# A graph network on one core: every third edge group permuted, a layer as one straight program, records in a ring

## The reference

```python
for l in range(6):
    W = ssp(edge_attr @ mlp_w1[l] + mlp_b1[l]) @ mlp_w2[l] + mlp_b2[l]   # ssp: softplus less log 2
    W = W * C[:, None]                       # cutoff from the edge's length
    xf = h @ conv_w1[l]
    msg = xf[src] * W
    agg = segment_sum(msg, dst, N)
    h = h + (ssp(agg @ conv_w2[l] + conv_b2[l]) @ lin_w[l] + lin_b[l])
x = layernorm(x + h)
for l in range(3):                           # second block
    z = (1 + eps[l]) * h + segment_sum(h[src], dst, n)
    h = relu(z @ W1[l] + b1[l]) @ W2[l] + b2[l]
```

## Time and profile before

| | |
|---|---|
| timed runs | 4567.78, 4573.64, 4575.24 us, median 4573.64 |
| profiled execution | span 6617.0 us |
| TensorE busy | 4785.2 us, 72% |
| its weight loads | 3558.4 us, 54% |
| VectorE | 3028.4 us, 46% |
| ScalarE | 2174.5 us, 33% |
| GpSimd | 2995.9 us, 45% |
| moved by DMA | 574.64 MB, 87 GB/s |

### The profile page before, as it was taken

How to read it: one execution, slowest core, us unless ns; L and a number is a source line. 1 busy time by engine, 2 the same in 40 slices (tenths; PEclk the granted TensorE clock), 3 DMA queues, 4 the chain that set the end, 5 groups by cost and what they waited for, 6 DMA issues and landing times.

```text
span 6617.0 us, 88816 instructions
## 1 busy us (share of the span) xinstructions
PE 4785.2 (72%) x24401; PEld 3558.4 (54%) x24684; DVE 3028.4 (46%) x8117; ACT 2174.5 (33%) x3585; POOL 2995.9 (45%) x3161
## 2 busy tenths in 40 slices
PE   0376777867777777777777777767777777777789
PEld 0365555645555555555555555545555555555544
DVE  3244444544444444444444444544444444444532
ACT  0133333333333333333333333333333333333322
POOL 5634444444454445444445444444445444445400
PEclk5687777777777777777777777777778777777799
DMA  4452233233233333233333323233333332323300
GB/s 157 137 151 84 83 86 88 82 91 85 82 87 85 85 90 89 80 86 86 86 86 91 85 84 88 85 85 87 85 85 88 86 89 84 86 84 87 87 14 9
DMA packets 324938, 574.64 MB, mean 87 GB/s; under 512 B 73578, under 2 KB 117300, under 8 KB 322996
## 3 DMA queue, kind: packets, MB, share of 16 engines
q1 hardware_dynamic: 202572, 357.07, 17.9%
q0 software_dynamic: 100160, 203.51, 11.5%
q10 hardware_dynamic: 21928, 11.64, 0.6%
HBM read 524.00 MB, written 47.93 MB: 86 GB/s over the span
## 4 chain that ended last, share of the span: by engine, by line
PE 40%; another core or an unknown queue 27%; issue 13%; DVE 10%; DVEq 4%; ACT 4%; POOL 2%; DMA 1%; ACTq 0%; SPq 0%; POOLq 0%
PE ps_w L680 10%; PE ps_h L781 9%; PE ps_a L695 8%; PE ps_a L692 4%; PE ps_pair L894 3%; POOL permuted L551 2%; DVE ex_msg L1428 2%; PE ps_pair L707 2%; DVEq L342 2%; ACT ps_w L1025 1%; DVE aggT L1409 1%; PE ps_a L669 1%; DVE phot L1388 1%; ACT xc L1062 1%
## 5 line engine op out<-in xcount | busy, mean ns | idle before, releaser
L561 POOL DMA_INDIRECT rows<-node_table,src_all x2982 | 2820.5, 946 | 3117.5 <-DVE ex_msg L1428 1937.8
L680 PEld LDWEIGHTS ps_w<-edge_w,hid 128*128 128x128 f32 x8064 | 1336.7, 242 | 1295.6 <-issue 1295.3
L680 PE MATMUL ps_w<-edge_w,hid 128*128 128x128 f32 x8064 | 1392.8, 329 | 719.0 <-ACT ps_w L1025 471.4
L1571 DVE SCALAR_TENSOR_TENSOR hid<-xc,ps_h 128x512 f32<-128x512 f32 x1008 | 690.9, 686 | 1859.5 <-remote 1328.5
L1060 ACT ACTIVATE xc<-ps_h 128x512 f32<-128x512 f32 x1008 | 601.3, 597 | 2648.2 <-remote 1363.6
L781 PE MATMUL ps_h<-buffers,edge_w 112*128 112x512 f32 x2016 | 1347.9, 756 | 86.4 <-DVE hid L1571 46.3
L695 PE MATMUL ps_a<-hot,ex_msg 128*128 128x32 f32 x6048 | 952.1, 306 | 469.7 <-issue 251.2
L695 PEld LDWEIGHTS ps_a<-hot,ex_msg 128*128 128x128 f32 x6048 | 887.8, 226 | 522.6 <-issue 512.8
L1062 ACT ACTIVATE xc<-xc,half_col 128x512 f32<-128x512 f32 x1008 | 727.3, 722 | 32.6
L1025 ACT COPY ps_w<-seed_rows 128x512 f32<-128x512 f32 x1008 | 591.6, 587 | 413.9 <-DVE ex_msg L1428 342.8
L1416 DVE TENSOR_TENSOR aggT<-aggT,ps_a 128x32 f32 x756 | 140.4, 186 | 927.2 <-remote 631.0
(11 more groups left out here) (236 smaller groups left out, 2825.5 us busy)
## 6 DMA issues: line engine op xcount, KB each, us to landing
buffers<-in_attr SPq DMA_DIRECT2D x756, 224.0 KB
buffers<-src_select SPq DMA_DIRECT2D x252, 256.0 KB
buffers<-attr_permuted SPq DMA_DIRECT2D x252, 224.0 KB
rows<-node_table,src_all POOLq DMA_INDIRECT x2982
permuted<-aggT SPq DMA_DIRECT2D x7, 1248.0 KB, 17.6
hid<-permuted SPq DMA_DIRECT2D x42, 208.0 KB
counts<-in_rec SPq DMA_DIRECT2D x4, 1924.0 KB, 35.4
hi_mid<-node_table SPq DMA_DIRECT2D x6, 1280.0 KB
```

Source lines behind the costliest of these rows:

```text
L561: pool.indirect_dma_start(out=rows[:, use % RS, t * F:(t + 1) * F], out_offset=None, in_=table[:, :], in_offset=bass.IndirectOffsetOnAxis( ...
L680: mm = pe.matmul(ps_w[u % 2][:, t * F:(t + 1) * F], hid[:, u % 2, t * P:(t + 1) * P], edge_w[:, EW_W2:EW_W2 + F], start=False, stop=(t == ...
L1571: dve.scalar_tensor_tensor(out=hid[:, i % 2, :], in0=xc[:, i % 2, :], scalar=LOG_MAX, in1=ps_h[i % 2][:, :], op0=ALU.min, op1=ALU.max).the ...
```

## The change

1. `M` is 3: every third group is permuted, 56 of 168 in a layer; 112 are gathered. The permuted tail of edges is 204 tiles, not 148, and 56 groups are turned in the prologue.
2. The loop over passes is gone: `U` = 168, and the engines' programs hold a whole layer, with constant addresses. The slice copies go. Early node chunks are tied to steps 72, 120 and 159, and the count tiles (27 groups of four in a layer, 28 before) are spread by `count_steps`, mostly over steps of unpermuted index.
3. `rows` has 7 slots; the edge features keep 4, now indexed apart from `M`; `select` keeps two, one for every other permuted group.
4. Records pass the scatter in a ring of three quarters of the tail: the load of the fourth quarter waits until the first is scattered. The zeroing is in 13 pieces.
5. For room, start tables (`pbase_i`, `block_i`, `base_i`, `pbase_kept`) share one buffer on different partitions, and `in_window` lies in `phot`.

```diff
-M = 4
-U = 24
+M = 3
+U = 168
-NIT = 7
-NP_GROUPS = NIT * J
-NQ_GROUPS = NIT * J * (M - 1)
+NP_GROUPS = J
+NQ_GROUPS = J * (M - 1)
-AS, RS = M, 6
+AS, RS = 4, 7
-CLEARS, REC_LOADS = 7, 4
+CLEARS, REC_LOADS, REC_RING = 13, 4, 3
-LEAD = M
-PRIME = 2
-EARLY_AT = [3, 5, 6]
+LEAD = 4
+PRIME = 4
+EARLY_STEP = [72, 120, 159]
-RANK_BLOCKS = 3
+RANK_BLOCKS = 2
-COUNT_STEP = [4, 4, 5, 6, 8, 9, 10, 11, 13, 13, 14, 15, 17, 18, 19, 20]
+def count_steps():
+    bounds, steps = [1] + EARLY_STEP + [U], []
+    room = [(end - first - 6) // 4 * 4 for first, end in zip(bounds, bounds[1:])][:EARLY]
+    wanted = [4 * round(BG * n / sum(room)) for n in room]
+    wanted[0] += BT - sum(wanted)
+    for first, end, n in zip(bounds, bounds[1:], wanted):
+        free = range(first + 3, end - 2)
+        light = [i for i in free if i % M]
+        heavy = [i for i in free if not i % M]
+        extra = n - len(light)
+        if extra > 0:
+            light += [heavy[j * len(heavy) // extra] for j in range(extra)]
+        else:
+            light = [light[j * len(light) // n] for j in range(n)]
+        steps += sorted(light)
+    return steps
+def group_of(use):
+    return use // (M - 1) * M + use % (M - 1) + 1
...
             for c in range(REC_LOADS):
-                part = slice(c * RT // REC_LOADS, (c + 1) * RT // REC_LOADS)
-                sp.dma_start(rec[:, part, :], rec_d[:, part, :]).then_inc(rec_in[c], 16)
+                first, end = REC_STARTS[c], REC_STARTS[c + 1]
+                if c >= REC_RING:
+                    wait_scattered(sp, c - REC_RING)
+                sp.dma_start(rec[:, c % REC_RING, 0:end - first, :], rec_d[:, first:end, :]).then_inc(rec_in[c], 16)
...
-            for t in range(RT):
-                if t in REC_STARTS:
-                    pool.wait_ge(rec_set, REC_STARTS.index(t) + 2)
-                    pool.sem_inc(gate, 1)
-                pool.indirect_dma_start(
-                    out=perm_d[:, :], out_offset=bass.IndirectOffsetOnAxis(ap=pos_i[:, t:t + 1], axis=0),
-                    in_=rec[:, t, :], in_offset=None).then_inc(scattered, 16)
+            for c in range(REC_LOADS):
+                pool.wait_ge(rec_set, c + 2)
+                pool.sem_inc(gate, 1)
+                for t in range(REC_STARTS[c], REC_STARTS[c + 1]):
+                    pool.indirect_dma_start(
+                        out=perm_d[:, :], out_offset=bass.IndirectOffsetOnAxis(ap=pos_i[:, t:t + 1], axis=0),
+                        in_=rec[:, c % REC_RING, t - REC_STARTS[c], :], in_offset=None).then_inc(scattered[c % REC_RING], 16)
...
+                    def gather_uses(first, last):
+                        for use in range(first, last):
+                            uses.wait(msg_done, group_of(use - RS))
+                            pool.sem_inc(gate, 1)
+                            gather_group(use, use, table_d[half])
...
                 with pe.Fori(0, K) as k:
-                    with pe.Fori(0, NIT) as it:
-                        uses = Uses(pe, layer * (K * NIT) + k * NIT + it).ready(-1, -5)
-                        early_step = load_early(pe, it)
-                        for i in range(U):
+                    uses = Uses(pe, layer * K + k).ready(-1, -5)
+                    for i in range(U):
+                        if i in EARLY_STEP:
+                            early_step = load_early(pe, EARLY_STEP.index(i))
...
-                                dve.tensor_scalar(phot[:, t, :], pwin_now[:, :], prel_now[:, first + t:first + t + 1],
+                        dve.tensor_scalar(phot[:, t, :], pwin_now[:, :], prel[:, first + t:first + t + 1],
...
-            def iteration_slices(it, n):
-                first, pfirst = it * ((U - J) * TPG), it * (J * TPG)
-                dve.tensor_copy(rel_now[:, :], rel[:, bass.ds(first, (U - J) * TPG)]).then_inc(slices_set, 1)
...
```

More of the change, by code:

```diff
@@ L54 @@
 EACH = -(-E // P)
-CLEARS, REC_LOADS = 7, 4
-REC_STARTS = [c * RT // REC_LOADS for c in range(REC_LOADS)]
+CLEARS, REC_LOADS, REC_RING = 13, 4, 3
+REC_STARTS = [c * RT // REC_LOADS for c in range(REC_LOADS + 1)]
+REC_MAX = -(-RT // REC_LOADS)
 CLEAR_PARTS = 16
@@ L93, with added_before @@
 GW_W1, GW_W2, GW_B1, GW_B2, GW_EPS, GW_N = 0, F, 2 * F, 2 * F + 1, 2 * F + 2, 2 * F + 3
-COUNT_STEP = [4, 4, 5, 6, 8, 9, 10, 11, 13, 13, 14, 15, 17, 18, 19, 20]
-assert len(COUNT_STEP) == BT
+def count_steps():
[14 more added lines that the diff above has]
+    return steps
+COUNT_STEP = count_steps()
+assert len(COUNT_STEP) == len(set(COUNT_STEP)) == BT
 def use_of(u):
     return u // M * (M - 1) + u % M - 1
+def group_of(use):
+    return use // (M - 1) * M + use % (M - 1) + 1
+def added_before(step):
+    return sum(not permuted(u) for u in range(step - ADD_LAG))
 def gathers_of(g):
@@ L492, in edge_loads @@
                 with sp.Fori(0, K) as k:
[L493 to L507, removed]
-                                             ).then_inc(attr_in[u % AS], 16)
-                                uses.wait(mm2_done, u - 2 * M)
-                                sp.dma_start(select[:, u // M % 2, :],
-                                             select_d[bass.ds(g, 1)].rearrange("a p t -> (a p) t")
-                                             ).then_inc(select_in[u // M % 2], 16)
-                            else:
-                                g = it * (J * (M - 1)) + use_of(u)
-                                sp.dma_start(attr[:, u % AS, :], attr_d[bass.ds(g, 1)].rearrange("a p t -> (a p) t")
-                                             ).then_inc(attr_in[u % AS], 16)
@@ new lines, in edge_loads @@
+                    uses = Uses(sp, layer * K + k).ready(-4, 0, 4)
+                    for u in range(U):
+                        if u == M:
+                            with sp.If(k < 1):
+                                rows_stored = sp.snap(layer * (16 * NCH) + 16 * NCH)
+                                rows_used = sp.snap(layer * (K * J) + PRIME)
+                                with sp.If(half > 0):
+                                    node_rows(1, rows_stored, rows_used)
+                                with sp.Else():
+                                    node_rows(0, rows_stored, rows_used)
+                        uses.wait(mm1_done, u - AS)
+                        if permuted(u):
+                            g = u // M
+                            sp.dma_start(attr[:, u % AS, :], attrp_d[g]
+                                         ).then_inc(attr_in[u % AS], 16)
+                            uses.wait(mm2_done, u - 2 * M)
+                            sp.dma_start(select[:, u // M % 2, :],
+                                         select_d[g]
+                                         ).then_inc(select_in[u // M % 2], 16)
+                        else:
+                            g = use_of(u)
+                            sp.dma_start(attr[:, u % AS, :], attr_d[g]
+                                         ).then_inc(attr_in[u % AS], 16)
```

366 lines of the change are left out of this document (169 added, 197 removed).

## The result

| | before | after |
|---|---|---|
| timed runs | 4567.78 to 4575.52 us | 4926.15, 4931.69, 4944.17, 4958.29 us |
| median | 4574.44 us | 4937.93 us |
| ratio | | 1.0802, 95% interval 1.0775 to 1.0829 |

The forecast was 4434 us, in a range of 4320 to 4600. The measured time lies outside it, on the other side. The profiled execution of after took 4926.15 us with a span of 4924.3, so it can be read without a correction. It is called the undisturbed profile.

The account below looks back on a forecast made before the run. GpSimd's gathers were taken to bound the kernel before, TensorE the kernel after. Prologue +120, layer 0 nothing, five layers with borders -240 and end -20 made -140: 4434 us, range 4320 to 4600.

Parts of the forecast that it names:

- TensorE's work: Edge loop: steps, 108 count tiles and 56 selects sum to 565 us a layer, 3.50 a step with waits.
- 4% for waits on other engines: Edge loop: added to TensorE's floor of 3.36 us a step, giving 3.50 a step, 588 us a layer.
- The floor and the pace: TensorE in the edge loop: at least 3.36 us a step, 3.50 expected with waits.
- The gathers: GpSimd's node-row gathers, 1.25 us apart: 441 a layer instead of 497, 551 us instead of 621.
- The sign that more of GpSimd's idle time would be put down to VectorE's message: Trace after: GpSimd, no longer the longest, would wait more for VectorE; no size given.
- Rival (b): Edge loop paced by VectorE's chain and the granted clock at 3.70 us a step: 4638 or 4840 us, chance 0.16.
- The chain of permuted additions: VectorE's four additions per permuted group: hidden behind TensorE's work, cost nothing; 265 us if that cover failed.
- The prologue: Before the edge loop: more scatters, turned groups and ranking add 120 us, between 100 and 130.
- The straight layer: Edge loop without passes: 36 pass ends go, worth nothing, at most 180 us; no cost in instruction fetching.
- Rival (d): Straight code starved of instructions: each engine stalls 4 us per 24 steps, 172 us on top, 4606; chance 0.05.
- Packets of instructions: Trace after: the count of instruction packets grows severalfold from 261, as all engines now stream.
- The sum's base: A layer of before with its border: 621 us of gathers plus 45 of GpSimd standing still.

Follow-up runs that it names:

- the spaced kernel: The changed kernel with four count tiles in four steps in a row, then at least one step without a tile; 4497.26 us, 0.9838 of the kernel before.
- e14: The changed kernel with ten throwaway TensorE products ahead of each count tile that has to wait for the last group's addition; 4731.61 us, 1.0336 of the kernel before.
- e9: The changed kernel unaltered, measured again beside the kernel before; 4938.08 us, 1.0792 of the kernel before.
- e10: The changed kernel with a step free of count tiles after each group of four, in the same set as e9; 4497.26 us, 0.9838 of the kernel before.
- e0: The kernel before, unchanged, run again for a profile; 4566.71 us.
- the undisturbed profile of before: A new profile of the unchanged kernel before, span 4564.5 us, standing in for the earlier one of 6617.0 us.
- e15: The changed kernel unaltered, measured beside e14; 4945.3 us, 1.0808 of the kernel before.
- e1: The same kernel as e10, in a set where all executions of the kernel before were far slower; 0.9397 of the kernel before.

## Why the prediction was wrong

- **The step that failed** is "TensorE's work": "108 count tiles ... x 0.49", and from it "3.50 a step". The tile's own 0.49 us was right. That nothing waits ahead of it was taken over from the kernel before, where the list of steps leaves room between groups. The diff replaced this list by a rule, and the rule's output (4, 5, 6, 7, 8, ...) was never worked out and set beside the addition at i + 2. I allowed 4% for waits on other engines; the spaced kernel's layer is 75 us shorter (661.9 to 586.7), of which 242.2 / 6 = 40 is this wait and the other 35 the half clock behind it, as far as e14 can tell, whose layer of 625.8 is 36 us under that of after. These 75 us are 13% of the floor of 565, where 4 was allowed for all waits together. In the whole kernel they cost 441 us (e9 to e10).
- **The floor and the pace** of TensorE were right once the tiles are spaced: 3.51 to 3.55 us a step over the six layers of e10, forecast 3.50.
- **The gathers** are still 1.25 us apart, and GpSimd did pace the kernel before: 40% of the chain of e0. The sign that more of GpSimd's idle time would be put down to VectorE's message came true, against the undisturbed profile of before and not the 1937.8 us of the earlier trace rows: 571.6 us in after and 110.4 in e10, where before had

```profile
POOL rows L561 <- DVE ex_msg L1428: 28.0, 35, 17.6
```

  Rival (b) said the pace was VectorE's chain and the clock. It had the sign, and of the changed kernel it is half true, but by another wait; of the kernel before it is refuted.
- **The chain of permuted additions**, costed at nothing with 265 us if the cover failed, waited 52.0 us in all (e10) and 55.0 (after), no more than the 54.2 of the undisturbed profile of before.
- **The prologue** was forecast at +120 and came to +110.8. The scatter issued 204 tiles in 199.6 us of work and 61.9 of issue, 1.28 each.
- **The straight layer**, costed at nothing: right inside a layer, wrong at its end, 42 us. VectorE's idle time ahead of a narrow addition with nothing in the profile that explains it, up to 4.5 us at a time in the undisturbed profile of before (first row), is at most 1.1 us in e10 (second row).

```profile
DVE aggT L1416 <- issue: 154.1, 84, 4.5
```

```profile
DVE aggT L1429 <- issue: 15.7, 18, 1.1
```

  Rival (d) had the mechanism and put it at the wrong place. I noticed that a jump costs 4 us on VectorE and asked only which jumps go, not which one is left on an engine that is now the bound. The Trainium skill ("Runtime: NRT & Kernel Launch", section on instruction fetch) says that a taken branch to a target outside the window has to fetch it. The 4.39 us at the one branch back agree, and so does the lack of such a gap inside the straight layer.
- **Packets of instructions**, said to grow severalfold from 261, came to 474 (232 + 242), not twice as many; by bytes they came to 5.78 MB, where before had 2.42 (with the 17 packets of q8, which the earlier trace rows leaves out), 2.4 times as much.
- **The sum's base** was off too. I took 45 + 621 = 666 us for a layer of before with its border, from GpSimd's standstill in a disturbed profile. In the undisturbed one the standstill is some 25 us at four of five borders,

```profile
1660.91 0.94 POOL L561 DMA_INDIRECT rows<-node_table,src_all  x1 [24.60 <-issue]
```

  and six layers and five borders are 3885.91 us, 651.5 for a layer with its border. The gain was thus 5 x 14.5 = 72 us too high. For the spaced kernel e10 against e0 the terms are: prologue +109 (forecast +120), five layers with their borders -144 (-240, of which 72 is the base and the rest the longer borders), the last layer 591.0 against 628.3, -37 (0), and the end +1 (-20). The sum is -71, where -140 was forecast. The base and the longer borders made the gain 96 us too high, and the other terms made it 27 too low. With the tiles spaced the method would so have missed by 69 us and stayed inside its range.

## What to carry to other kernels

When a hand-written list of steps is replaced by a rule, write out what the rule gives and check each shared buffer against it: who frees it, in which step of that engine, and at which end of the step. On an engine that is about to become the bound, a wait costs its length and then the clock; a short wait that recurs may cost about twice its length, as it did here: 2.3 us of waiting and 2.1 of half clock. A gain on one engine is only realised by the next one's schedule, which has to be read as closely as the part that is changed; and the spaced kernel, 1.6% faster than before, shows that the idea was good and its companion edit was not.

## What the hardware showed that was not expected

- Idle times of TensorE of 2.2 to 2.8 us cost the clock. Behind 86, 88 and 94 of the 102 waits for `counts` (after, e9, e15) the granted clock went to the level of 1.2 GHz at once or within 2.5 us. The clock over the loop is 0.93 with these waits, and 0.98 both without them (e10) and with the same waits filled (e14).
- On the pausing chip TensorE's results come late now and then, with nothing in the profile that explains it. In e1, the spaced kernel there, the first row is TensorE's first product of a step, the second ScalarE's exponential that waits for it, which in the trace of after begins 0.6 us (median) after the start of the product's second half:

```profile
2009.85 1.10 PE L802 MATMUL ps_h<-buffers,edge_w 112*128 112x512 f32 x2
...
2015.64 0.60 ACT L1075 ACTIVATE xc<-ps_h 128x512 f32<-128x512 f32 x1 [5.76 <-issue]
```

The list of waits of e1 sums them up as the first row, where e10, the same kernel on the quiet chip, has the second:

```profile
ACT xc L1075 <- remote: 1503.9, 279, 13.0
```

```profile
ACT xc L1075 <- PE ps_h L802: 1182.2, 927, 3.4
```

These are the rows that made the profile of before so long. In e1 the long ones are mostly 10 to 30 us apart. The same kernel takes 6235 us there and 4497 on the quiet chip. The transfers are not the cause as far as the trace shows: a scatter of the prologue lands 2.2 us (median) after its issue in both e1 and after. What the pauses are, whether they belong to a chip, and why the spaced kernel gains 6 to 8% there and 1.6% on the quiet chip, stays open.
